# Quantised convolution block: second images' high bytes on GpSimd, first product on whole integers, one maximum per stage

## The reference, cut to what matters

```python
def _quant_act(x):
    qmax = 2.0 ** (QUANT_BITS - 1) - 1.0
    scale = jnp.maximum(jnp.max(jnp.abs(x)), 1e-12) / qmax
    return jnp.round(x / scale) * scale
residual = x
h = _shift_conv(x, w1)                                    # 1x1, 256 -> 64
h = _shift_conv(h, peg_w, pad=1, groups=64, bias=peg_b)   # 3x3, by channel
h = jax.nn.relu(_bn(h, ...))
h = _shift_conv(h, w2, pad=1)                             # 3x3, 64 -> 64
h = jax.nn.relu(_bn(h, ...))
h = _bn(_shift_conv(h, w3), ...)                          # 1x1, 64 -> 256
return jax.nn.relu(h + residual)
```

## Time and profile before

| what | value |
| --- | --- |
| runs, median (lowest to highest) | 92.92 us (92.44 to 93.06), 3 runs |
| profiled execution, its own time | 93.05 us |
| span in the profile | 91.3 us |
| busy: PE, PE weight loads, DVE, ACT, POOL | 75.5, 51.3, 67.0, 51.1, 5.0 us |
| mean granted PE clock | 0.982 of full speed |

### The profile page before, as it was taken

The page is one execution under the profiler, slowest core; times in us unless marked ns, Lnnn a source line. Parts: engine busy times, 40 slices in busy tenths (PEclk is TensorE's granted clock), DMA queues, the critical chain, the costliest instruction groups (busy, mean ns, idle before and its releaser), DMA issues.

```text
span 91.3 us, 2176 instructions
## 1 busy us (share of the span) xinstructions
PE 75.5 (83%) x886; PEld 51.3 (56%) x886; DVE 67.0 (73%) x182; ACT 51.1 (56%) x92; POOL 5.0 (6%) x10
## 2 busy tenths in 40 slices
PE   4999999995899898999999989967359889896400
PEld 1325665564798878798996964452214385572100
DVE  1225449999999599995799437977898875849950
ACT  4102374879948999994792015336363343744760
POOL 7500110000000000000003100000000000000000
PEclk9999999999999999999999999999999999999975
DMA  1999800000000000000000000000000000000076
GB/s 21 317 337 292 334 4 0 0 0 7 0 7 0 0 7 0 7 7 0 0 7 0 0 0 7 0 0 0 0 0 0 0 0 0 7 4 0 0 245 215
DMA packets 3274, 4.17 MB, mean 46 GB/s; under 512 B 256, under 2 KB 2688, under 8 KB 3264
## 3 DMA queue, kind: packets, MB, share of 16 engines
q1 hardware_dynamic: 2992, 3.76, 12.8%
q10 hardware_dynamic: 272, 0.26, 0.8%
HBM read 2.98 MB, written 1.05 MB: 44 GB/s over the span
## 4 chain that ended last, share of the span: by engine, by line
PE 49%; DVE 32%; ACT 10%; issue 4%; DVEq 0%; ACTq 0%
PE acc L475 15%; PE slot L462 9%; DVE g_rows L886 8%; PE slot L354 6%; PE acc L604 5%; PE acc L365 3%; DVE g_cols L1040 3%; PE slot L390 3%; ACT g_cols L704 2%; DVE g_cols L984 2%; ACT g_cols L788 2%; PE slot L539 2%; ACT pad L757 2%; DVE g_cols L1130 2%; DVE stats L948 2%
## 5 line engine op out<-in xcount | busy, mean ns | idle before, releaser
L886 DVE TENSOR_TENSOR g_rows<-hats 128x2304 f32<-128x2304 f32 (+1 forms) x12 | 20.6, 1752 | 0.1
L704 ACT ACTIVATE g_cols<-slot 128x768 f32<-128x768 f32 x24 | 17.8, 830 | 3.7 <-PE slot L462 3.7
L475 PE MATMUL acc<-g_cols,v_sb 128*64 128x128 f32 x288 | 17.9, 277 | 0.0
L475 PEld LDWEIGHTS acc<-g_cols,v_sb 128*64 128x64 f32 x288 | 15.5, 137 | 1.1 <-issue 0.3
L354 PE MATMUL slot<-zeros 128*128 128x512 bf16 x54 | 15.1, 412 | 1.2 <-DVE zeros L807 1.2
L462 PE MATMUL slot<-consts_sb,g_rows 64*128 64x64 f32 x288 | 11.8, 226 | 2.1 <-DVE g_rows L886 1.7
L462 PEld LDWEIGHTS slot<-consts_sb,g_rows 64*128 64x128 f32 x288 | 10.3, 139 | 3.9 <-DVE g_rows L886 2.6
L354 PEld LDWEIGHTS slot<-zeros 128*128 128x128 bf16 x54 | 5.4, 107 | 7.3 <-issue 2.6
L757 ACT ACTIVATE pad<-g_cols 64x256 bf16<-64x256 int8 x8 | 3.3, 418 | 4.6 <-DVE g_cols L1040 4.5
L817 DVE BATCH_NORM_STATS2 stats<-acc 128x6 f32<-128x256 f32 x4 | 1.7, 428 | 5.2 <-PE acc L365 2.6
L539 PE MATMUL slot<-consts_sb,mx 128*128 128x128 f32 x12 | 3.2, 319 | 2.3 <-DVE mx L991 2.0
(11 more groups left out here) (140 smaller groups left out, 117.6 us busy)
## 6 DMA issues: line engine op xcount, KB each, us to landing
out<-g_cols SPq DMA_DIRECT2D x4, 256.0 KB, 2.3
x_sb<-x SPq DMA_DIRECT2D x3, 256.0 KB, 4.4
wq_sb<-wq SPq DMA_DIRECT2D x1, 484.5 KB, 6.3
woff_sb<-woff SPq DMA_DIRECT2D x1, 288.0 KB, 5.5
w_sb<-w SPq DMA_DIRECT2D x1, 288.0 KB, 5.5
x_sb<-x ACTq DMA_DIRECT2D x1, 256.0 KB, 3.1
w_sb<-w SPq DMA_DIRECT2D x1, 256.0 KB, 6.4
consts_sb<-consts SPq DMA_DIRECT2D x1, 232.0 KB, 5.4
```

The source lines that it names most:

```text
L475: mm = nc.tensor.matmul(acc[b2][rows(h), at:at + P], v_sb[:, B2 * h + b2, q, k, :], g_cols[t][h][:, NQ * k + q, :], start=(k == 0 and q == ...
L704: nc.scalar.activation(dst.rearrange("p k (r n) -> p k r n", r=HALVES), src.rearrange("p r (k n) -> p k r n", k=per), ACT.Copy).then_inc(g ...
L886: tt(g_rows[i % 3][:, taps], hats[:, t, h, 1, taps].unsqueeze(3).to_broadcast(shape), hats[:, t, h, 0, taps].unsqueeze(2).to_broadcast(sha ...
```

## The change

1. **High bytes.** In stages 2 to 4 ACT casts only the high byte of the lower partitions (the first image of the pair). The second image's high byte is made by POOL, with a `tensor_scalar` (times 256) of 64 x 256 int8 to bf16, six instructions in all. POOL waits for the quotient, and from the second instruction on for its own last one. PE waits for `hi_by_pool` too, and so does DVE ahead of the first quotients of stages 3 and 4.
2. **Stage 1 on whole integers.** The byte casts of stage 1 are gone. The 1.5 * 2^23 is subtracted in place, by ACT for three of the four quotients and by DVE for the last, and PE multiplies float32 by float32 weights (`w1q`, a new DVE product of 128 x 128 beside `wqb`): four products per pair, where there were eight in bf16. Of the two runs of idle matmuls between low and high parts, those between the pairs (two matmuls) stay.
3. **One maximum per stage.** Stage 1 reduces both pairs at once and spreads once (`first_half_max(1)` and one `spread_max` are gone; the four idle matmuls more keep PE busy instead). In stages 3 and 4 the second pair's `raw` starts its maximum from the first pair's, and there is one spread of 128 columns, one bias product of 128 columns instead of 256, and one scale over 128 columns instead of 256. Stage 2 keeps two maxima.
4. **Order on ACT.** `root4(1)` comes ahead of `relu0(0)`.

```diff
@@ gpsimd, after pegq
+            pool.wait_ge(pads_zero, 3)
+            pool.wait_ge(placed, 1)
+            q2 = quot[:, 0, 0].rearrange("p b n -> p (b n)")
+            for n in (2, 3, 4):
+                for b2 in range(B2):
+                    pool.wait_ge(quot_ready, CH * B2 + B2 * (n - 2) + b2 + 1)
+                    if n > 2 or b2 > 0:
+                        pool.wait_ge(hi_by_pool, B2 * (n - 2) + b2)
+                    src = byte(q2[rows(1), N * b2:N * b2 + N], 1, I8)
+                    dst = inner(pads[n - 2][CB:P, b2], 1) if n < 4 else n4[CB:P, b2, 1, :]
+                    nc.gpsimd.tensor_scalar(dst, image(src) if n < 4 else src, 256.0, None, ALU.mult
+                                            ).then_inc(hi_by_pool, 1)
@@ tensor
-            spread_max(1, 0)
-            idle(IDLE[7], slot[0][:, BANK:2 * BANK])
-            spread_max(1, 1)
+            idle(IDLE[7] + 4, slot[0][:, BANK:2 * BANK])
+            spread_max(1)
...
+                if b2 == 1:
+                    idle(IDLE[15], spare)
+                for c in range(CH):
+                    if (b2, c) == LAST_WHOLE:
+                        pe.wait_ge(whole_by_dve, 1)
+                    else:
+                        pe.wait_ge(whole_by_act, CH * b2 + c + 1)
+                    for h in range(HALVES):
+                        mm = nc.tensor.matmul(acc[b2][rows(h), 0:N], w1q[:, CB * c:CB * c + CB],
+                                              quot[:, c, b2, h, :], start=(c == 0), stop=(c == CH - 1))
@@ scalar
             norm3(0, (1, 2))
+            root4(1)
             relu0(0)
-            root4(1)
...
-                    high_part(flat(n1_hi[:, c, b2]), byte(flat(quot[:, c, b2]), 1, I8), CH * b2 + c + 1)
+                    if (b2, c) != LAST_WHOLE:
+                        a.wait_ge(quot_ready, CH * b2 + c + 1)
+                        q1 = flat(quot[:, c, b2])
+                        nc.scalar.activation(q1, q1, ACT.Identity, bias=minus_round[:, 0:1]).then_inc(whole_by_act, 1)
@@ vector
+            tt(w1q[:], wq_mag[:, Q_W1:Q_W1 + CH * CB], wq_sign[:, Q_W1:Q_W1 + CH * CB], ALU.mult).then_inc(wq_ready, 1)
...
-            first_half_max(1, LEAST_MAX)
...
-                if i > 0:
-                    low1(i - 1)
-            low1(B2 * CH - 1)
+            dve.wait_ge(quot_ready, CH * B2)
+            last_q = flat(quot[:, CH - 1, B2 - 1])
+            ts(last_q, last_q, ROUND, None, ALU.subtract).then_inc(whole_by_dve, 1)
...
+                    least = mx[:, n, b2 - 1:b2] if b2 > 0 else bn_minus[:, n - 3:n - 2]
+                    if b2 > 0:
+                        dve.wait_ge(raw_ready, B2 * (n - 3) + b2)
...
-                make_scale_of_both(n)
+                make_scale(n, least_scale[:, 0:1])
```

More of the change, by code:

```diff
@@ L84 @@
 ROUND = 1.5 * 2.0 ** 23
+LAST_WHOLE = (1, 1)
 SQRT2 = 1.4142135623730951
@@ L147, in build @@
         wqb = sb("wqb", [P, Q_COLS], BF16)
+        w1q = sb("w1q", [P, CH * CB])
         pegq = sb("pegq", [P, TAPS, CB], BF16)
@@ L299, in sums_of, with spread_of @@
             return acc[0][:, N:N + 8] if n == 3 else small[b2][:, 0:8]
-        spread = [small[0][:, P + P * b2:2 * P + P * b2] for b2 in range(B2)]
+        SPREADS = (0, 1, 3, 4, 5)
+        def spread_of(n, b2):
+            return small[b2][:, P:2 * P]
         def rows(h):
@@ L530, in eight_vars, with spread_max @@
                                  ).then_inc(sq_done, 1)
-            def spread_max(n, b2):
+            def spread_max(n, b2=0):
                 biased = n >= 3
                 if biased:
-                    pe.wait_ge(raw_ready, B2 * (n - 3) + b2 + 1)
+                    pe.wait_ge(raw_ready, B2 * (n - 2))
                 else:
-                    pe.wait_ge(max_ready, B2 * (n - 1) + b2 + 1)
-                nc.tensor.matmul(spread[b2] if biased else small[b2][:, P:2 * P],
-                                 mx[:, n, b2:b2 + 1].to_broadcast([P, P]), ident, start=not biased, stop=True, is_transpose=not biased,
+                    pe.wait_ge(max_ready, SPREADS[n] - (n == 2 and b2 == 0))
+                nc.tensor.matmul(spread_of(n, b2), mx[:, n, (b2, B2 - 1)[biased]:(b2, B2 - 1)[biased] + 1].to_broadcast([P, P]), ident,
+                                 start=not biased, stop=True, is_transpose=not biased,
                                  skip_group_check=True).then_inc(max_spread, 1)
@@ L545, in spread_bias @@
                 pe.wait_ge(quot_ready, CH * B2 + B2 * (n - 3) + 1)
-                nc.tensor.matmul(small[0][:, P:P + B2 * P].rearrange("p (b n) -> p b n", b=B2),
-                                 bn_off[:, n - 3:n - 2].to_broadcast([P, P]),
-                                 ident.unsqueeze(1).to_broadcast([P, B2, P]),
+                nc.tensor.matmul(spread_of(n, 0), bn_off[:, n - 3:n - 2].to_broadcast([P, P]), ident,
                                  start=True, stop=False, skip_group_check=True)
@@ L592, in parts_ready @@
             def parts_ready(n, b2):
-                pe.wait_ge(lo_ready, CH * B2 + HALVES * (B2 * (n - 2) + b2 + 1))
-                pe.wait_ge(hi_ready, CH * B2 + HALVES * (B2 * (n - 2) + b2 + 1))
+                done = B2 * (n - 2) + b2 + 1
+                pe.wait_ge(lo_ready, HALVES * done)
+                pe.wait_ge(hi_ready, done)
+                pe.wait_ge(hi_by_pool, done)
             def window_conv(weights, pad, n):
@@ L769, in high_parts @@
                 for b2 in range(B2):
-                    for h in range(HALVES):
-                        src = byte(q2[rows(h), N * b2:N * b2 + N], 1, I8)
-                        high_part(dst(b2, h), image(src) if n < 4 else src, CH * B2 + B2 * (n - 2) + b2 + 1)
+                    src = byte(q2[rows(0), N * b2:N * b2 + N], 1, I8)
+                    high_part(dst(b2, 0), image(src) if n < 4 else src, CH * B2 + B2 * (n - 2) + b2 + 1)
             a.wait_ge(pads_zero, 3)
@@ L811, in _ @@
             nc.vector.memset(one_sb[:], 1.0)
+            nc.vector.memset(minus_round[:], -ROUND)
             dve.wait_ge(first_in, 16)
```

61 lines of the change are left out of this document (24 added, 37 removed).

## The result

The changed kernel takes 93.58 us (median of 15 runs) against 93.06 of the kernel before: ratio 1.0054, 95% interval 1.0034 to 1.0073. It is 0.5 us slower; 91.6 had been forecast, with a range from 91.1 to 93.4. The profiled execution took 93.4 us, with a span of 91.5.

What follows compares the result with a forecast made beforehand. The prediction took one path hopping between PE, DVE and ACT as the bound. Its terms, -0.38 - 0.39 + 0.20 - 0.50 - 0.26 = -1.33 us, gave 91.7 from the profiled 93.05, 91.6 in the runs; range 91.1 to 93.4.

Steps and rivals of the forecast that it cites:

- A: End of the first block: the square ahead of the clamp on ACT starts earlier, the clamp stays hidden; -0.38 us.
- B: Stage 1: with one maximum, the second pair's first residual follows DVE's piece by 0.57 instead of 0.96 us; -0.39 us.
- E: Stages 3 and 4: the scale over fewer columns takes 350 instead of 484 ns, twice -0.13; -0.26 us.
- C: Stage 1 on whole integers: the maximum starts near 70.30 instead of 70.09; +0.20 us, likely ends -0.1 and +0.4.
- D: High bytes shared with POOL: -0.25 us each in stages 2 and 3, nothing gained in stage 4; -0.50 us.
- The sign that I had named for this: Stage 4: if its casts stretch, the prediction fails altogether, since nothing hides them.
- Rival 1: Stages 2 to 4: POOL and DVE take turns, total -1.33 + 6m; 93.3 us at m = 0.30; chance 0.33.
- m: The time POOL's high byte holds DVE up per pair; 6m on the path over three stages.
- Rival 2: POOL is slow but alone (0.69 us or more): D shrinks to -0.24, 91.9 us; at 0.9 us +0.2, 92.3; chance 0.10.
- Rivals 3 and 4: 3: first block's gains fail, ACT late, 92.1 us, chance 0.10. 4: POOL's first `tensor_scalar` costs microseconds to start, chance 0.02.

Runs made afterwards that it cites:

- e9: The changed kernel without parts 1, 2 and 4, so one maximum per stage alone, against the kernel before: ratio 0.9931.
- e8: The changed kernel without part 1 and without the two zero matmuls between the pairs of stage 1: ratio 0.9846 to the kernel before.
- e6: The kernel before with ten POOL instructions on scratch tiles near its start: two multiplications took 1.76 us, two casts of the same bytes 0.74.
- e4: The kernel before with the change's six POOL instructions added, writing to scratch tiles that nobody on the path waits for: ratio 1.0119.
- e14: Repeat of the changed kernel with stage 1 in bytes, POOL casting in stages 2 and 3 only, 256 in the weights: ratio 0.9860 to before.
- e10: The changed kernel with stage 1 in bytes and POOL casting instead of multiplying in stages 2 to 4, 256 in the weights: ratio 0.9890 to before.
- e12: The kernel before with six POOL plain casts added, to scratch tiles that nobody on the path waits for: one execution, 94.37 us.

## Why the prediction was wrong

- **A, order on ACT: right.** -0.38 forecast, -0.45 measured (e9). The square at 60.25, the clamp hidden behind the root.
- **B, one maximum: right.** -0.39 forecast, -0.39 measured (e9), the 0.57 of the first pair exactly. The eight-number reduction cost nothing.
- **E, narrower scales: right.** -0.26 forecast, -0.24 to -0.26 measured (C3, C4).
- **C, stage 1: right sign, too small.** +0.20 forecast, +0.50 measured. The product itself was sized right, 1.08 us from its start against 0.86 and 0.21. Two pieces were not: PE to DVE took 0.13 (68.26 + 1.08 = 69.34, reduction at 69.47), which I left out though the row of before has 0.11 there; and the product behind the zero matmuls began 0.16 later than in my sum. I had the two zero matmuls in the sum and did not see that they could be dropped, which takes S1 from 4.24 to 3.73 (e8).
- **D, high bytes: the step that failed.** I took -0.50 and said of stage 4 that nothing was gained and nothing lost. Measured: +1.12. The step that failed is the overlap: I took POOL's instruction as hidden behind DVE's casts, and DVE's queue as untouched by it. Both were wrong. POOL's instruction was sized from the copy (0.40) and from slopes (0.51 to 0.69; the 0.86 ns a column behind the 0.18 and the 0.69 stands in no row); the operation itself takes 0.85 (e6), beyond my whole bound, because the copy's pace doesn't hold for arithmetic, and the two-input product's 2.0 ns a column wasn't its ceiling. And DVE's instructions beside it get slower, which is where most of it went: 0.84 (e4). The sign that I had named for this came: the casts of stage 4 stretched, and nothing hid them. Even with POOL's cast, which is done ahead of DVE's, stages 2 and 3 gained 0.16 each (e14), not 0.25.
- **The rivals.** Rival 1 had the place right (DVE's queue, no cover in stage 4) and, with its m at 0.27 (-0.50 + 6m = 1.12), a time close to the one measured: it gave 93.3 at m = 0.30 (its own sum makes 93.4). That closeness is in part luck: DVE alone lost 0.84 over six instructions of POOL, an m of 0.14, which by the rival's sum is 92.4. The rest came from what the rival's sum had otherwise: the gain of 0.50 that it still counts didn't come, PE's wait for POOL cost 0.28, and stage 1 took 0.3 more. It had 0.33 of the chances, and I chose the sum without it although the casts' double rate was evidence for the rule and nothing in the trace was evidence against. The mechanism is softer than taking turns: DVE isn't held for POOL's 0.85 us. A pair of casts loses 0.08 to 0.10 us in stages 2 and 3, the two pairs of stage 4 lose 0.34 and 0.07, and the instruction of two columns 0.17. Rival 2 was right beside it: POOL's instruction took up to 0.95 us in stages 2 and 3, and of D's cost 0.28 was the wait for it, where the rival at 0.9 us had +0.2. Rivals 3 and 4 didn't happen: POOL's first `tensor_scalar` started 0.20 us behind its quotient (71.78 against 71.10 + 0.48).
- **The range** ended at 93.4 because I took m = 0.30 for its end, with C at +0.20, and added no lateness of POOL on top; DVE's loss, POOL's lateness and C's further 0.3 came together.

**The rule.** What was slowed and what wasn't, changed kernel against before: stage 3's second quotient, read from SBUF beside POOL, took 0.42 us (the four of before have a mean of 0.35), in the timeline after:

```profile
78.06 0.42 DVE L1057 TENSOR_SCALAR g_cols<-act,q_inv 128x256 f32<-128x256 f32 x1
```

Stage 2's quotients, read from PSUM, of which the second began 0.3 us before POOL was done, stayed at the 0.48 of before; in the groups by form after (busy us, mean ns, idle before):

```profile
L1057 DVE TENSOR_SCALAR g_cols<-acc,q_inv 128x256 f32<-128x256 f32 x2 | 1.0, 483 | 0.1
```

The Trainium skill, "SBUF — State Buffer", section "Who interferes with whom", says that casts and `tensor_scalar` on DVE contend with GpSimd when they run in a mode that uses both port pairs, and that an instruction with at most one SBUF input outside these modes doesn't. For the casts and the quotients the runs agree: those from SBUF were stretched, the quotient from PSUM, which takes 0.48 us for the columns that take 0.35 from SBUF, was not. A product of two single columns beside POOL kept its 0.16 us too (79.25, with POOL until 79.52).

The runs don't agree on the price: by the same section of the Trainium skill the instruction that comes second blocks until the first one is done, which would be up to 0.85 us. In stage 2 after, POOL's first instruction ends at 72.63 (71.78 + 0.85), and both of DVE's casts beside it are done at 72.33 (71.62 + 0.71). The first of them, begun ahead of POOL, kept its 0.29 us, and the second, begun behind POOL, took 0.39. In stage 4, where POOL began ahead of both, they took 0.48 and 0.42. The measurement decides; why the price is what it is stays open.

## What to carry to other kernels

Work moved to POOL can slow the DVE work that stays. Beside DVE's casts and `tensor_scalar` between SBUF tensors both engines got slower here, so put POOL's work beside DVE instructions that read PSUM or have slack, and never beside the stretch where DVE alone is the path. On POOL the cast of 64 x 256 is less than half as long as the multiplication (0.40 against 0.85 us); fold the factor into weights that are made once. And when an engine's own work grows, look first for the idle matmuls next to it.

## What the runs showed of the hardware that I had not expected

- POOL's `tensor_scalar` of 64 x 256 takes 0.85 us for int8 and float32 inputs, bf16 and float32 outputs, flat or as an image; its cast takes 0.39 to 0.40 (e6).
- The slowing goes both ways: POOL's cast takes 0.40 alone and 0.40 to 0.53 beside DVE's casts (e10, e14), its multiplication 0.85 alone and 0.85 to 0.95 beside them. A DVE instruction of two columns beside POOL took 0.40 us, 0.23 before.
- In one execution PE's clock was at its lower level for more than 3 us in stage 1, which cost 0.5 us there (e12); another execution, as little busy ahead of it (0.53 of 2 us), kept the higher one (before).
- The first product of the kernel took 1.08 to 1.98 us in executions of code that is the same on PE up to there.
